# Neighbour-mean layers: both products ahead of the edge sum, from one transpose, with the product gathered; and one bias folded into the next behind the GCN sum

## The reference

```python
# layer L3, the graph part: two mean layers
def _sage_conv(x, src, dst, W_l, b_l, W_r):
    gathered = jnp.take(x, src, axis=0)
    summed = jax.ops.segment_sum(gathered, dst, num_segments=N_NODES)
    deg = jax.ops.segment_sum(jnp.ones_like(dst, dtype=x.dtype), dst, num_segments=N_NODES)
    mean_nb = summed / jnp.maximum(deg, 1.0)[:, None]
    return mean_nb @ W_l + b_l + x @ W_r
h = jax.nn.relu(_sage_conv(x, src, dst, W1_l, b1, W1_r))
h = _sage_conv(h, src, dst, W2_l, b2, W2_r)

# layer L2, the graph part: behind the weighted sum over the edges
h7 = jax.ops.segment_sum(msgs, row_sl, num_segments=N) + b
h = jax.nn.relu(h7 @ W1 + b1)
out = h @ W2 + b2
```

## Time and profile before

| | |
|---|---|
| median of three runs | 6503.13 us |
| the profiled execution, its time | 6501.18 us |
| its span in the trace | 6499.0 us |
| TensorE busy | 4718.4 us, 73% |
| VectorE busy | 3611.8 us, 56% |
| ScalarE busy | 2538.9 us, 39% |
| GpSimd busy | 3699.6 us, 57% |
| granted TensorE clock, mean | 0.815 of full speed |

### The profile page before, as it was taken

One profiled execution on the slowest core, in us unless ns is written; L12 is line 12 of the kernel. 1 busy time (PEld: TensorE's weight loads), 2 busy tenths in 40 slices (PEclk: granted clock), 3 DMA queues, 4 the chain that ended last, 5 costly groups with the idle time before them and its releaser, 6 DMA issues. The chain is left out here.

```text
span 6499.0 us, 108814 instructions
## 1 busy us (share of the span) xinstructions
PE 4718.4 (73%) x21790; PEld 3703.7 (57%) x21791; DVE 3611.8 (56%) x12643; ACT 2538.9 (39%) x8675; POOL 3699.6 (57%) x3788
## 2 busy tenths in 40 slices
PE   3976664886788788576777888868655565556997
PEld 1544443675666666465555788867533354335876
DVE  7998887326555555647887444452455445544112
ACT  0975551115998899424554311112200010002222
POOL 4107771574775777374776477754277757771221
PEclk8989996997888788698999655559877777777998
DMA  2013332223344344333333111122233323342445
GB/s 53 3 33 102 103 102 64 79 55 115 106 106 92 101 106 106 72 110 120 104 104 84 27 8 8 8 19 78 93 105 105 105 65 105 105 100 84 176 170 175
DMA packets 300058, 562.04 MB, mean 86 GB/s; under 512 B 84760, under 2 KB 178626, under 8 KB 299586
## 3 DMA queue, kind: packets, MB, share of 16 engines
q0 software_dynamic: 167008, 401.55, 24.6%
q1 hardware_dynamic: 119852, 146.38, 6.9%
q10 hardware_dynamic: 13110, 13.08, 0.6%
HBM read 491.05 MB, written 69.70 MB: 86 GB/s over the span
## 5 line engine op out<-in xcount | busy, mean ns | idle before, releaser
L1080 PE MATMUL psM<-G,S 128*128 128x257 f32 (+3 forms) x6080 | 1939.2, 456 | 984.0 <-DMA G<-table_ones,ids 596.5
L1080 PEld LDWEIGHTS psM<-G,S 128*128 128x128 f32 x6080 | 1329.9, 251 | 1408.3 <-DVE acc L1111 620.5
L1111 DVE TENSOR_TENSOR acc<-acc,psM 128x257 f32 (+3 forms) x3068 | 1152.5, 376 | 1010.2 <-PE psM L1080 841.2
L1005 POOL DMA_INDIRECT G<-table_ones,ids x1248 | 1195.0, 958 | 757.9 <-ACT ids L952 402.4
L1005 POOL DMA_INDIRECT G<-table_gat,ids x840 | 809.6, 964 | 266.2 <-issue 252.4
L963 ACT ACTIVATE G<-G 128x64 f32<-128x64 f32 x3360 | 824.7, 333 | 6.8
L1005 POOL DMA_INDIRECT G<-table_ffn_gat,ids x548 | 521.3, 951 | 175.0 <-issue 144.7
L1579 DVE TENSOR_TENSOR ys<-psY,b2b 128x256 f32<-128x256 f32 x248 | 105.3, 425 | 801.2 <-PE psY L1518 746.7
L1459 POOL DMA_INDIRECT out_by_choice<-ys,to_choice x248 | 247.5, 998 | 526.3 <-DVE ys L1579 471.1
L1032 PEld LDWEIGHTS psE<-AD,St 128*128 128x128 f32 x2800 | 510.8, 263 | 27.8 <-issue 6.6
L1005 POOL DMA_INDIRECT G<-table_gcn,ids x416 | 400.5, 963 | 194.0 <-issue 125.8
(11 more groups left out here) (381 smaller groups left out, 7106.9 us busy)
## 6 DMA issues: line engine op xcount, KB each, us to landing
w1s<-in_L_ffn_W SPq DMA_DIRECT2D x32, 1024.0 KB, 8.9
w2s<-in_L_ffn_W SPq DMA_DIRECT2D x32, 1024.0 KB, 5.9
G<-table_ones,ids POOLq DMA_INDIRECT x1248, 2.8
land<-out_by_choice SPq DMA_DIRECT2D x75, 256.0 KB, 3.1
G<-table_gat,ids POOLq DMA_INDIRECT x840
rows_by_token<-XN SPq DMA_DIRECT2D x20, 640.0 KB, 3.3
G<-table_ffn_gat,ids POOLq DMA_INDIRECT x548, 2.4
G<-table_gcn,ids POOLq DMA_INDIRECT x416
```

What stands on the lines that cost most here:

```text
L1005: pool.indirect_dma_start(G[:, g, j, :], None, table, bass.IndirectOffsetOnAxis(ids[:, g, j:j + 1], 0)).then_inc(gathered[g], 16)
L1080: nc.tensor.matmul(psM[:, j, 0:W], S[:, g, j, :], G[:, g, j, :], start=True, stop=True).then_inc(summed, 1)
L1111: nc.vector.tensor_tensor(ab, ab, psM[:, n0 % EG, 0:W], ALU.add).then_inc(added, 1)
```

## The change

- sage1 takes both products of a tile from one transpose: the weights for the own row and for the neighbours lie side by side (`wgt["sage1"]`, 512 wide), `keep` copies the first half into TR and the second into XN (`also`), and the table is XN, the product, stored once it is kept. GpSimd adds the bias to TR behind the kept group (`pool_back`).
- sage2 loses the `first` path. VectorE forms acc times 1/degree plus TR in one instruction for each tile (`joined`), and relu for the group. The product is again 512 wide. GpSimd adds the second bias to X first, and then TR to X behind each kept group.
- ffn3 loses the `first` path and GpSimd's additions: VectorE forms acc times 1/degree plus X for each tile (`joined_into_x`).
- gatf: the bias of the sum goes through W1 once (four products one column wide into psH, an addition on VectorE into the next bias), ahead of everything else of the block; TensorE waits for it, and `copy_a` becomes one plain copy.
- Two more semaphores in every dense, one more in layer L3, which moves the places where spent ones are cleared.

```diff
@@ dense
+                folded = first is not None and first.hid is not None
+                bias_out, bias_ready = sem("bias_out"), sem("bias_ready")
@@ gpsimd
+                        if pool_back is not None:
+                            for t0, t1 in groups:
+                                pool.wait_ge(kept, t1)
+                                pool_back(t0, t1).then_inc(pooled, 1)
@@ tensor
+                        if folded:
+                            for h in range(KD):
+                                for k in range(KD):
+                                    m = nc.tensor.matmul(psH[:, h, 0:1], first.hid[0][:, k, h * P:(h + 1) * P], first.col[:, k:k + 1],
+                                                         start=(k == 0), stop=(k == KD - 1))
+                            m.then_inc(bias_out, 1)
+                            pe.wait_ge(bias_ready, 1)
@@ scalar
-                            if first.col is None:
+                            if first.col is None or folded:
                                 nc.scalar.copy(ats[:, t % 4, :, :].rearrange("p k n -> p (k n)"), psA[:, t % 2, 0:D]).then_inc(copied_a, 1)
@@
                         def keep(t):
                             act.wait_ge(multd, t + 1)
-                            nc.scalar.activation(into(t), psL[:, t % RL, 0:W[1]], ACT.Copy,
-                                                 scale=1.0 if scale is None else scale[:, t:t + 1]).then_inc(kept, 1)
+                            if also is not None:
+                                nc.scalar.copy(into(t), psL[:, t % RL, 0:D])
+                                nc.scalar.copy(also(t), psL[:, t % RL, D:2 * D]).then_inc(kept, 1)
+                            else:
...
@@ vector
+                        if folded:
+                            dve.wait_ge(bias_out, 1)
+                            nc.vector.tensor_tensor(first.hid[1][:, :], first.hid[1][:, :], psH[:, 0:KD, 0], ALU.add).then_inc(bias_ready, 1)
                         if first is not None:
                             widen(0)
@@ layer L3
             def add_sage2(pool):
                 for t0, t1 in FIVES:
...
+                m.then_inc(biased, 1)
+                pool.wait_ge(biased, 1)
...
+            def joined(link, t0, t1):
+                for t in range(t0, t1):
+                    m = nc.vector.scalar_tensor_tensor(out=XN[:, t, 0:D], in0=acc[:, t, 0:D], scalar=rdeg[:, t:t + 1], in1=TR[:, t, :],
+                                                       op0=ALU.mult, op1=ALU.add)
+                link(m)
+                return nc.vector.tensor_scalar(XN[:, t0:t1, 0:D], XN[:, t0:t1, 0:D], 0.0, None, ALU.max)
+
+            def joined_into_x(link, t0, t1):
+                for t in range(t0, t1):
+                    m = nc.vector.scalar_tensor_tensor(out=X[:, t, :], in0=acc[:, t, 0:D], scalar=rdeg[:, t:t + 1], in1=X[:, t, :],
+                                                       op0=ALU.mult, op1=ALU.add)
+                return m
-            dense("sage1", SHORT_END, xn_row, got=True, W=(wgt["sage_r1"], D), into=own_row, tables=[(tab1[1], XN, D, "rows")])
+            dense("sage1", SHORT_END, xn_row, got=True, W=(wgt["sage1"], 2 * D), into=own_row, also=xn_row, pool_back=add_sage1, tables=[(tab1[1], XN, D, "kept")])
             edge_sum("sage1", LB, tab1[1], W1TAB, acc, zeros_in(acc, W1TAB))
-            dense("sage2", FIVES, xn_row, ln=False, fold=in_degrees, first=First(acc_row3, acc_group3, rdeg, None, None, wgt["sage_l1"], joined, relu_rows),
-                  pool_front=add_sage1, beside=add_sage2, W=(wgt["sage_r2"], D), into=own_row, tables=[(tab1[2], XN, D, "rows")])
+            dense("sage2", FIVES, xn_row, ln=False, fold=in_degrees, front=joined, beside=add_sage2, pool_back=add_own,
+                  W=(wgt["sage2"], 2 * D), into=own_row, also=xn_row, tables=[(tab1[2], XN, D, "kept")])
             edge_sum("sage2", LB, tab1[2], W1TAB, acc, zeros_in(acc, W1TAB))
-            dense("ffn3", FIVES, xn_row, fold=in_degrees, first=First(acc_row3, acc_group3, rdeg, None, None, wgt["sage_l2"], to_x3, None),
-                  pool_front=add_own, small=(wgt["gate3"], 8, LG, [row["gate3"][:, :]]), tables=[(XD, XN, D, "rows")])
+            dense("ffn3", FIVES, xn_row, fold=in_degrees, front=joined_into_x, small=(wgt["gate3"], 8, LG, [row["gate3"][:, :]]), tables=[(XD, XN, D, "rows")])
```

More of the change, by code:

```diff
@@ L154, in program @@
         shapes = {"gat1": WGAT + HEADS, "gat2": WGAT + HEADS, "gatf": 24, "gcn": D, "gcn1": D, "gcn2": D,
-                  "sage_r1": D, "sage_l1": D, "sage_r2": D, "sage_l2": D, "gate0": 8, "gate1": 8, "gate3": 8}
+                  "sage1": 2 * D, "sage2": 2 * D, "gate0": 8, "gate1": 8, "gate3": 8}
         wgt = {n: sb(f"w_{n}", [P, KD, w]) for n, w in shapes.items()}
@@ L557, in dense @@
         def dense(name, groups, rows, ln=True, got=None, front=None, first=None, col=None, W=None, scale=None, into=None,
-                  small=None, tables=(), att=None, fold=None, degrees=None, beside=None, pool_front=None):
+                  small=None, tables=(), att=None, fold=None, degrees=None, beside=None, pool_front=None, pool_back=None, also=None):
             LAG = 9 if first is not None else 0
@@ L727, in fire @@
                         def fire(t):
+                            if t == 0:
+                                act.wait_ge(bias_ready, 1)
                             act.wait_ge(hidden, t + 1)
@@ L748, in keep @@
                             act.wait_ge(multd, t + 1)
-                            nc.scalar.activation(into(t), psL[:, t % RL, 0:W[1]], ACT.Copy,
-                                                 scale=1.0 if scale is None else scale[:, t:t + 1]).then_inc(kept, 1)
+                            if also is not None:
+                                nc.scalar.copy(into(t), psL[:, t % RL, 0:D])
+                                nc.scalar.copy(also(t), psL[:, t % RL, D:2 * D]).then_inc(kept, 1)
+                            else:
+                                nc.scalar.activation(into(t), psL[:, t % RL, 0:W[1]], ACT.Copy,
+                                                     scale=1.0 if scale is None else scale[:, t:t + 1]).then_inc(kept, 1)
                         if degrees is not None:
@@ L1818, in program @@
             rdeg = sb("rdeg", [P, NT])
[L1820 to L1824, removed]
+            biased = sem("biased")
             def in_degrees(link):
@@ L1831, in own_row @@
                 return TR[:, t, :]
-            def joined(t, ps):
-                return nc.vector.tensor_tensor(XN[:, t, 0:D], TR[:, t, :], ps, ALU.add)
-            def relu_rows(t0, t1):
-                return nc.vector.tensor_scalar(XN[:, t0:t1, 0:D], XN[:, t0:t1, 0:D], 0.0, None, ALU.max)
             def add_sage1(t0, t1):
@@ L1843, in add_sage2 @@
                 for t0, t1 in FIVES:
-                    nc.gpsimd.tensor_tensor(X[:, t0:t1, :], X[:, t0:t1, :], wide(row["sage2"][:, :], t1 - t0), ALU.add)
+                    m = nc.gpsimd.tensor_tensor(X[:, t0:t1, :], X[:, t0:t1, :], wide(row["sage2"][:, :], t1 - t0), ALU.add)
+                m.then_inc(biased, 1)
+                pool.wait_ge(biased, 1)
             def add_own(t0, t1):
                 return nc.gpsimd.tensor_tensor(X[:, t0:t1, :], X[:, t0:t1, :], TR[:, t0:t1, :], ALU.add)
-            def to_x3(t, ps):
-                return nc.vector.tensor_tensor(X[:, t, :], X[:, t, :], ps, ALU.add)
```

4 lines of the change are left out of this document (2 added, 2 removed).

## The result

The changed kernel takes 6479.15 us (median of 7 runs, 6472.14 to 6486.93), beside 6501.95 for the kernel before in the same session: the ratio is 0.9967, with an interval of 0.9955 to 0.9979. It was timed once more, on another chip: 6481.01 beside 6500.94, ratio 0.9968 (0.9956 to 0.9981). One more run by itself took 6487.49, beside 6501.43 for the kernel before. The forecast was 6480.

What follows compares the result with a forecast made beforehand. Stages run in turn: VectorE's combining paces sage1, TensorE bounds sage2, both stall in ffn3. Terms 12.4 + 1.5 - 4.6 - 34.3 + 1.5 = -23.5 us from 6501.18, plus 1.95 to the median, give 6480; range 6464 to 6493.

Steps and rivals of the forecast that it cites:

- The product's price: sage1 and sage2, TensorE: a 512-wide product takes twice a 256-wide one, 1.71 us, and a tile 1.93.
- The root loop: sage1: a group waits for ScalarE's root, behind copies that wait for TensorE; groups of five take 11.2 us, not 9.1.
- GpSimd's additions ... nothing: sage1: additions of 2.9 us, one a group, fall at VectorE's statistics and cost nothing.
- the slot of 6.5 for the group of two: sage1's end: 6.5 us from the group of three to the group of two.
- the tail, 8.2 with the keeps: sage1's end: 7.3 us for the last group's two transposes and last four products, 0.9 for the keeps.
- up to 7 more if the clock falls: sage1's upper bound: up to 7 us more if the clock falls at each of four stalls of 1.6 us.
- the first group, 10.0: sage1: first group takes 10.0 us, with three products ahead of its fifth transpose and 2.3 more for the lower clock.
- the upper end between 3.7 and 17.5: sage2: first group ready at 17.5 us instead of some 3.7, VectorE's joined instructions each standing behind a GpSimd addition.
- The copies without bias: gatf: ScalarE's copies are 0.25 us shorter, easing four stalls at group ends and the first tile, some -1.4.
- the second: Rival, sage1: clock falls at the stalls or a GpSimd addition meets VectorE's combining each group; 5 to 8 more, near 6487; chance 0.16.
- The other three terms: Stage terms besides sage1's: sage2 -4.6 us, ffn3 -34.3, gatf +1.5.
- the slower case: Rival, sage1 and sage2: TensorE at 1.2 GHz through the doubled products; slower once mean clock is below 0.80; chance 0.07.

Runs made afterwards that it cites:

- the run with gatf's order: Changed kernel with VectorE's first gatf widening ahead of its wait for the tiny products and bias addition: 7594.25 us, where the kernel before takes 7612.65.
- the run without the bias: Changed kernel with the bias of the first mean layer left out, so GpSimd adds nothing to TR in sage1: one run at 6470.29 us.
- the runs with the bias later: Changed kernel with GpSimd's additions of the bias to X in sage2 started only after VectorE joined all groups: 6464.56 us, ratio 0.9946.
- the run in halves: Changed kernel with each of GpSimd's five bias additions to X in sage2 split into two over half the columns: one run at 6480.18 us.
- the clearings moved: Changed kernel with the folded bias's two semaphores made only in gatf's block, so clearings fall where they did before the change: 6477.98 us.
- the version with the three orders: Changed kernel with sage2's bias behind the joining, sage1's root one tile earlier, gatf's first widening ahead of the wait: 7569.64 us (0.9947); elsewhere 6457.10 (0.9935).

## Why the prediction was right, and where it wasn't

**The product's price: right.** Twice a 256-wide one, 1.72, and a tile 1.94, where 1.71 and 1.93 were worked out from one step of widths.

**sage1: right in kind, 5 to 7 us too small** in the three profiles, and 3 in the run with gatf's order, where the clock stayed up. The root loop gave 11.37 a group where 11.2 was said, and moving the root took it away. The failed steps, by the profiled run (predicted 61.8 with the clearing, measured 68.4):
- "GpSimd's additions ... nothing" and the slot of 6.5 for the group of two: 8.76. Of the 2.3, 1.7 is the addition on which VectorE's normalising waited, as the run without the bias showed. I had checked the additions against VectorE's statistics for full groups only. The other 0.5 I put down to ScalarE's order, where the root of the last group stands behind the store of the fourth; that was argued, not tried by itself.
- the tail, 8.2 with the keeps: 9.9. The stall of 2.73 ended at 1.2 GHz: 3.09 for a product of 1.88. The bound "up to 7 more if the clock falls" held this; it fell at one stall, the last of five.
- the first group, 10.0: 11.26 in this run, 10.3 and 10.4 in the two others. It was between 9.7 and 11.3 over eight profiles, by how long the first product ran at 1.2 GHz (2.67 to 3.62 us, and at 3.62 the second was slow too). The 10.0 of the sum lies 0.3 above the shortest and 1.3 below the longest. Why the clock rises sooner in one run than in another is not shown.
- the rest: 0.4 over the other groups, the clearing of semaphores 2.0 instead of 1.5 (1.5 and 1.7 in the two other profiles), and 0.5 at the last store, which now leaves only when the last tile is kept.

**sage2: right.** 74.1 said, 73.6 to 74.5 measured, and by its own steps: 2.90 for the degrees, 12.13 for five joined instructions, the first transpose at 17.3, then TensorE. The choice of the upper end between 3.7 and 17.5 is confirmed from both sides by the runs with the bias later (4 us, stage 12 to 13 less) and with half additions. The rule of the Trainium skill (SBUF — State Buffer, Who interferes with whom) that spoke against this change holds in this case: a vector instruction with two SBUF inputs stands behind a whole instruction of GpSimd. What the run in halves adds is that the two take turns when both have a queue: the cost is one GpSimd instruction for each of these instructions of VectorE.

**ffn3: right.** 43.3 said, 43.0 in three profiles; groups 6.03 apart against 6.1.

**gatf: the mechanism right, the net not shown.** The first transpose was late by 2.8, for the reason given, and putting the widening first took 2.3 of it back. The two widenings took 6.37 us where some 3 each were said:

```profile
3567.77 6.37 DVE L813 TENSOR_TENSOR acc<-acc,DINV 128x1280 f32<-128x1280 f32 x2
```

But three profiles give 85.7, 84.1 and 84.5 against 84.4, and all ten with gatf in this order 83.5 to 85.7. So most of the 2.8 comes back later. The copies without bias were to give back 1.4; whether they gave the rest too, no run tells apart. Against the one profile of before the term is -0.9 to +1.3 instead of +1.5, and the folded bias bought no time that these runs can show.

**The sum.** The stages give -18 to -20, the medians -22.8 and -19.9; the forecast was -23.5. So the single number was lucky by 3 to 6 us against the stages: the medians fell by up to 5 us more than these, in parts that scatter. Of the rivals, the second (sage1 loses more, 5 to 8) is nearest to what happened in its stage, though not as it was put: the clock fell at one stall and not at each, and one addition, not one a group, met VectorE's normalising and not its combining. The other three terms made 1 to 2 us of it up. But for the first products of a stage and those behind the last stall, TensorE ran at full clock through the doubled products, so the slower case had no ground. From the first transpose of sage1 on, before and after:

```profile
4654.00:4703.00 49.00, 34.11 (x150) 26.89 (x150) 35.41 (x109) 17.91 (x55) 0.00 (x0) 0.87 0.42 131
```

```profile
4660.00:4729.00 69.00, 54.66 (x150) 24.95 (x150) 36.70 (x107) 24.44 (x80) 14.63 (x6) 0.92 0.29 93
5290.00:5306.00 16.00, 16.00 (x50) 7.64 (x49) 2.81 (x6) 7.89 (x27) 4.46 (x2) 1.00 0.16 56
5873.00:5916.00 43.00, 30.46 (x150) 29.71 (x150) 30.39 (x108) 10.50 (x30) 0.00 (x0) 0.53 0.22 77
```

The columns are as in the earlier trace rows, and the second block is the changed kernel's: granted clock 0.92 in sage1 where it was 0.87, 1.00 in the middle of sage2, and 0.53 in ffn3, where TensorE's small products have slack beside VectorE until the tail. The 0.77 that the prediction took for sage1's average spans 26 us ahead of the first transpose, where TensorE was busy for 0.21 us at a granted 0.56; it was a weak ground for the slower case.

## What to carry to other kernels

A product that is moved from a stage to the one before it is paid there in full (20 to 26 us for 25 tiles, of which TensorE's 25 x 0.86 are 21.5) and returns more than itself (31 to 35 us) when it takes transposes, copies and widenings with it; but then the host stage is TensorE's, and everything ahead of its first transpose counts in full. So put side work of GpSimd behind the instructions of VectorE that start such a stage, or cut it small, and take a root or any other step of a loop one tile ahead of the copies that wait for TensorE: three changes of order gave as much (23.9 us) as the whole change (19.9). Check the short groups at the end by themselves: there one event can start a store, a root and an addition at once.

## What the runs showed of the hardware that I had not expected

- VectorE and GpSimd take turns by instruction. Beside additions of 2.9 to 3.1 us five instructions that take 2.05 us alone take 12.13, beside ones of half the width 8.03; an instruction on 128x25 elements takes 2.90 or 1.55 instead of 0.18. Not every instruction waits: the reciprocal of 128x25 ran beside an addition in its usual 0.32.
- GpSimd's first addition comes 7.3 us behind its configuration (5257.5 to 5264.8 without the additions of sage1, as in the earlier trace rows) and at once (5264.57, with the block) in the changed kernel, where additions ran in sage1, with only indirect DMAs in between; there the configuration stands in sage1, at 4648.0. The Trainium skill (GPSIMD Engine Reference, Instruction dispatch) gives some 6 us for code that is loaded at a first call; the gap here is 7.3. That delay can protect VectorE: it made sage2 some 12 us shorter.
- Eight profiles hold sage1 with the change's own order. After the same stall of 2.7 us TensorE went on at 1.2 GHz in six (products of 3.08 to 3.28) and at 2.4 GHz in two (1.88 with the clearings moved; and the run with gatf's order). Those two also have the shortest first groups, 9.79 and 9.69 us against 9.97 to 11.29. After stalls of 1.45 the clock never fell. The length of the stall doesn't decide alone: in the kernel before the product behind a stall of 2.74 took its full-clock 1.03 us, while behind one of 2.03 the products took 1.19 and 1.92.
- One chip took 7612.65 us for what takes 6500 on the others. The dense stages were equal within 2 us. Each of the two edge sums of layer L3 took 107 to 114 us more; moving the same 562.01 MB, the version with the three orders showed there:

```profile
DMA packets 300056, 562.01 MB, mean 74 GB/s; under 512 B 84760, under 2 KB 178626, under 8 KB 299586
```

where the page of the changed kernel on the usual chip has 87 GB/s. The gain in microseconds was the same on both chips (43.0 and 43.8), so its ratio is nearer to 1 on the slow one (0.9947 and 0.9935; the two intervals overlap, so it is the stages that show it).
